# Edge set-up in parts between the pairs, more comparisons on the scalar engine, diagonals ahead: a graph layer and expert kernel

## The reference

```python
# x: 3125 x 256, src, dst: 50000 edges sorted by dst, edge_weight: 50000
def _gcn_conv(h, row, col, ew, dis, W, b):
    xw = h @ W
    norm = dis[row] * ew * dis[col]
    msg = norm[:, None] * xw[row]
    agg = jax.ops.segment_sum(msg, col, num_segments=N)
    return agg + (dis * dis)[:, None] * xw + b

x = x + gnn(layernorm(x))          # two layers: conv, layernorm, relu, residual
x = x + moe(layernorm(x))          # 16 experts, the best 2 of each row, then layernorm
```

## Time and profile before

| | us |
|---|---|
| median of 3 runs | 1250.4 (1247.85 to 1251.97) |
| profiled execution | 1253.59 |
| its span, first to last instruction | 1251.9 |
| PE busy | 1102.1 (88%) |
| DVE busy | 720.1 (58%) |
| ACT busy | 341.6 (27%) |
| POOL busy | 608.7 (49%) |

### The profile page before, as it was taken

The page is one execution under the profiler, slowest core; times in us unless marked ns, Lnnn a source line. Parts: engine busy times, 40 slices in busy tenths (PEclk is TensorE's granted clock), DMA queues, the critical chain, the costliest instruction groups (busy, mean ns, idle before and its releaser), DMA issues. The chain is left out here.

```text
span 1251.9 us, 19252 instructions
## 1 busy us (share of the span) xinstructions
PE 1102.1 (88%) x6433; PEld 952.7 (76%) x6436; DVE 720.1 (58%) x1970; ACT 341.6 (27%) x794; POOL 608.7 (49%) x625
## 2 busy tenths in 40 slices
PE   1675789799999999997799999999994599999967
PEld 1453568588888888886588888888883599999954
DVE  8978668903444444342427777777777355454536
ACT  1538332401111121111101111111211133343337
POOL 3777777777777777770001111111112355555525
PEclk9999978799999999998899999999996799999988
DMA  7999700033433433213045544535447422222236
GB/s 282 335 392 389 309 2 1 8 106 106 157 107 117 147 107 111 101 54 105 0 176 178 202 155 150 202 126 193 146 146 247 145 73 73 69 73 73 72 106 234
DMA packets 76335, 180.75 MB, mean 144 GB/s; under 512 B 28930, under 2 KB 58252, under 8 KB 66508
## 3 DMA queue, kind: packets, MB, share of 16 engines
q1 hardware_dynamic: 44984, 151.67, 33.6%
q0 software_dynamic: 19776, 15.76, 4.6%
q10 hardware_dynamic: 11476, 12.07, 3.0%
HBM read 122.12 MB, written 57.33 MB: 143 GB/s over the span
## 5 line engine op out<-in xcount | busy, mean ns | idle before, releaser
L458 POOL DMA_INDIRECT weights_by_cell<-w_cell,cell x391 | 413.0, 1056 | 140.5 <-issue 136.1
L1148 PE MATMUL ps<-x_rows,w 128*128 128x256 f32 x1300 | 296.4, 383 | 7.4 <-DMA w<-weights_by_cell 7.1
L1148 PE MATMUL ps<-w 128*128 128x256 f32 x1300 | 301.1, 385 | 1.1 <-ACT w L850 1.1
L1148 PEld LDWEIGHTS ps<-x_rows,w 128*128 128x128 f32 x1300 | 248.0, 192 | 41.2 <-DMA w<-weights_by_cell 7.9
L1148 PEld LDWEIGHTS ps<-w 128*128 128x128 f32 x1300 | 243.4, 192 | 32.7 <-ACT w L850 2.6
L508 POOL DMA_INDIRECT token_and_home_of_slot<-pair,slot_id x50 | 49.6, 992 | 346.7 <-DVE slot_id L779 339.1
L606 DVE TENSOR_TENSOR layer<-ps,w 128x1024 bf16<-128x1024 f32 x87 | 105.0, 1216 | 26.2 <-PE ps L987 26.1
L1466 DVE TENSOR_SCALAR hidt<-ps,b1t 128x128 f32<-128x128 f32 x232 | 65.3, 344 | 90.6 <-PE ps L1322 90.6
L1334 PE MATMUL ps<-w,hidt 128*128 (+1 forms) x464 | 109.8, 380 | 0.0
L1322 PEld LDWEIGHTS ps<-xt,w1s 128*128 128x128 f32 x880 | 106.9, 192 | 2.8
L1322 PE MATMUL ps<-xt,w1s 128*128 128x128 f32 x880 | 107.1, 275 | 0.0
(11 more groups left out here) (237 smaller groups left out, 1371.3 us busy)
## 6 DMA issues: line engine op xcount, KB each, us to landing
w<-weights_by_cell SPq DMA_DIRECT2D x49, 1600.0 KB, 6.9
weights_by_cell<-w SPq DMA_DIRECT2D x26, 1600.0 KB, 8.4
w<-in_L_ffn_w_dram SPq DMA_DIRECT2D x32, 512.0 KB, 8.8
weights_by_cell<-w_cell,cell POOLq DMA_INDIRECT x391
w<-in_x_dram ACTq DMA_DIRECT2D x1, 3072.0 KB
hot<-in_x_dram ACTq DMA_DIRECT2D x24, 128.0 KB, 2.1
normalised_rows<-hot ACTq DMA_DIRECT2D x24, 128.0 KB, 4.7
out_dram<-w SPq DMA_DIRECT2D x24, 128.0 KB
```

The costliest lines, as they stand in the source:

```text
L458: pool.indirect_dma_start(adj[:, :], bass.IndirectOffsetOnAxis(ap=cell[0:m, c:c + 1].bitcast(U32), axis=0), w_cell[0:m, n, half * CH + j:h ...
L1148: mm = pe.matmul(bank(k % 2, 0, D), ring[:, place_of(k), s * P:(s + 1) * P], tab[q][:, s, :], start=(s == 0), stop=(s == NT - 1))
```

## The change

- The set-up before pair 0 is for group 0 alone, after small loads of its own; the other three groups are made in 25 steps each (`part`), two steps a pair from pairs 4, 17 and 30 on. The limits are made after pair 1, and GpSimd waits for `part_ready` of the group that it scatters.
- ScalarE compares 23 pairs: 20, 24 to 44 in steps of four, and 50, 53 to 95 in steps of three (L61's rule gave 11). It has a bank of its own (2) and a fourth buffer; VectorE has two banks and three buffers. TensorE makes the key rows for ScalarE's next pair right after its present one.
- The turns and products start at s=100 (84 before), the scaling by dis at s=177, spread over the rest; the normalisation is at s=46 to 94, every fourth s.
- SP waits on the scatters' semaphores (`seconds`), not on GpSimd's count `placed`. The blank is half as long and read twice. Loads and GpSimd's first instructions are reordered.
- `combine` has twelve diagonals ahead, four in their own memory and eight in the experts' weight buffer; the gates are made in expert block 6, and in `combine` ScalarE makes halves of diagonals at 7/6 a tile.

```diff
-KBANKS = 3
+KBANKS, ACT_BANK = 2, 2
...
-ACT_FIRST, ACT_LAST, ACT_STEP = 20, 64, 4
+P_MEAN, P_PASSED, P_SHIFT, P_DEG = 14, 14, 22, HOT_LAST + 4
+T_APPLY, APPLY_STEP, T_TAB, TAB_STEP, T_DEG = 46, 4, 100, 3, 2 * P_DEG
+T_SCALE = max(2 * P_DEG + 6, T_TAB + TAB_STEP * NT + 2)
+P_GUARD = T_APPLY // 2 + 2
+
+ACT_PAIRS = tuple(range(20, 48, 4)) + tuple(range(50, PAIRED - 1, 3))
+DVE_PAIRS = tuple(p for p in range(PAIRED) if p not in ACT_PAIRS)
+SIDE, PART_OPS, PART_SPAN = 6, 24, 13
+SECONDS = 16 * (CH * ((CHUNKS + 1) // 2) - 1)


 def by_act(p):
-    return ACT_FIRST <= p < ACT_LAST and (p - ACT_FIRST) % ACT_STEP == 0
-
-
-def act_pairs(p):
-    return sum(by_act(k) for k in range(p))
+    return p in ACT_PAIRS
+
+
+def part_pair(g, j):
+
+    return 4 + (g - 1) * PART_SPAN + j // 2 + (j >= SIDE)

...
-                sp.dma_start(e_int[0:SH, 0:SG - 1, :], dst[0:full * SBE].rearrange("(g s e) -> s g e", s=SH, e=SBE)).then_inc(edges_in, 16)
+                sp.dma_start(e_int[0:SH, 0, :], dst[0:SH * SBE].rearrange("(s e) -> s e", e=SBE)).then_inc(edges_first, 16)
                 for half in range(2):
-                    sp.dma_start(e_w[half * SH:(half + 1) * SH, 0:SG - 1, :],
-                                 edge_weight[0:full * SBE].rearrange("(g s h q) -> h s g q", s=SH, h=2, q=P)[half]).then_inc(weights_in, 16)
...
-                        sp.reg_load(reg, chunks_of[0:1, t:t + 1])
-                        sp.wait_ge(placed, sp.snap(reg, min_val=1, max_val=CHUNKS + 1))
+                        for j in range(2):
+                            sp.reg_load(regs[j], second_need[0:1, j, t:t + 1])
+                        for j in range(2):
+                            sp.wait_ge(seconds[j], sp.snap(regs[j], min_val=16 * CH, max_val=SECONDS))
+                            sp.sem_inc(cells_blank, 1)
...
+                        pool.wait_ge(part_ready, (n * CH + CH - 1) // SH + 1)
                         pool.wait_ge(w_ready, n + 1)
...
-                        pool.sem_inc(placed, 1)
-                n = CHUNKS - 1
-                pool.wait_ge(seconds[n % 2], 16 * (CH * (n // 2 + 1) - 1))
-                pool.sem_inc(placed, 1)
+                pool.wait_ge(seconds[0], SECONDS)
+                pool.wait_ge(seconds[1], 16 * CH * (CHUNKS // 2))
...
-                dve.wait_ge(ends_ready, 1)
-                dve.tensor_scalar(key_part[:, :, :], e_f, MID, None, ALU.subtract).then_inc(keys_ready, 1)
-                ew = e_w.rearrange("p g q -> p (g q)")
-                dve.wait_ge(weights_in, 16 * 5)
-                link(dve.tensor_scalar(bad_e, ew, 0.0, 0.0, ALU.mult, ALU.not_equal))
-                link(dve.copy_predicated(ew, bad_e, zeros[:, :]))
-                link(dve.scalar_tensor_tensor(ew, ew, -1.0, ew, ALU.mult, ALU.max))
-                dve.tensor_scalar(ew, ew, 1e-6, None, ALU.max).then_inc(weights_ready, 1)
+                def part(g, j):
+
+                    at = (3 if g == 0 else 7) * BANK
+                    ends_ps = ps[:, at:at + 2 * P].rearrange("p (h t s) -> p h t s", h=2, t=2)
+                    dst_ps, src_ps = ends_ps[:, :, 0, :], ends_ps[:, :, 1, :]
...
+                    elif j == 17:
+                        link(dve.tensor_copy(w_parts[:, 0, cols], w_ps))
+                    elif j == 18:
+                        link(dve.tensor_tensor(rest, w_ps, w_parts[:, 0, cols], ALU.subtract))
+                    elif j == 19:
+                        link(dve.tensor_copy(w_parts[:, 1, cols], rest))
+                    elif j == 20:
+                        dve.tensor_tensor(w_parts[:, 2, cols], rest, w_parts[:, 1, cols], ALU.subtract).then_inc(cols_ready, 1)
...
-                    dve.wait_ge(keyrow_ps, p + 1)
-                    if p >= MRING:
-                        dve.wait_ge(wsum_ps, 2 * (p - MRING) + 2)
+                    d = DVE_PAIRS.index(p)
+                    dve.wait_ge(keyrow_ps, d + 1)
+                    if d >= MRING:
+                        dve.wait_ge(wsum_ps, 2 * DVE_PAIRS[d - MRING] + 2)
...
+                    for g in range(1, SG):
+                        for j in range(PART_OPS + 1):
+                            if part_pair(g, j) == p:
+                                part(g, j)
...
                 pair(1)
-                link(dve.tensor_copy(work_i[:, :], dst_c))
-                link(dve.tensor_scalar(work_i[:, :], work_i[:, :], 7, None, ALU.logical_shift_right))
-                link(dve.tensor_copy(dst_hi, work_i[:, :]))
+                limits()
                 weigh(0)
-                link(dve.scalar_tensor_tensor(dst_lo, dst_hi, -float(P), dst_c, ALU.mult, ALU.add))
+                limits_back()
+                for j in range(21, PART_OPS + 1):
+                    part(0, j)
...
                 def act_compare(p):
-                    act.wait_ge(keyrow_ps, p + 1)
-                    if act_pairs(p):
-                        act.wait_ge(same_by_act, act_pairs(p))
+                    a = ACT_PAIRS.index(p)
+                    act.wait_ge(part_ready, 2 * p // SH + 1)
+                    act.wait_ge(keyrow_act, a + 1)
+                    if a:
+                        act.wait_ge(same_by_act, a)
                     for k in range(2):
                         for half in range(2):
...
-                    act.activation(same[:, p % MRING, :, :, :].rearrange("p s h q -> p (s h q)"),
+                            act.activation(key_gap[:, k, half, :], bank(ACT_BANK, k * SBE, (k + 1) * SBE), ACT.Abs,
+                                           bias=key[:, c:c + 1], scale=-1.0).then_inc(apart, 1)
+                    act.wait_ge(apart, 4 * (a + 1))
+                    if a:
+                        act.wait_ge(wsum_ps, 2 * ACT_PAIRS[a - 1] + 2)
+                    act.activation(same[:, MRING, :, :, :].rearrange("p s h q -> p (s h q)"),
                                    key_gap.rearrange("p s h q -> p (s h q)"), ACT.Relu, bias=ones_f[:, 0:1], scale=-1.0).then_inc(same_by_act, 1)
...
                         if t > 0:
                             take_product(t - 1)
...
+                    if s >= T_SCALE:
+                        if s == T_SCALE:
+                            act.wait_ge(dis_ready, 1)
+                            act.wait_ge(prod_read, NT)
+                        for t in range((s - T_SCALE) * NT // (SBS - T_SCALE), (s + 1 - T_SCALE) * NT // (SBS - T_SCALE)):
                             act.activation(tab[0][:, t, :], tab[0][:, t, :], ACT.Copy, scale=dis[:, t:t + 1]).then_inc(tab_ready[0], 1)

...
+                def next_key_rows(p):
+
+                    wait_same(p)
+                    if by_act(p):
+                        a = ACT_PAIRS.index(p) + 1
+                        if a < len(ACT_PAIRS):
+                            key_rows(ACT_PAIRS[a], ACT_BANK, keyrow_act)
+                    else:
+                        d = DVE_PAIRS.index(p) + KBANKS
+                        if d < len(DVE_PAIRS):
+                            key_rows(DVE_PAIRS[d], d % KBANKS, keyrow_ps)
+                    if p == ACT_PAIRS[0] - 4:
+                        key_rows(ACT_PAIRS[0], ACT_BANK, keyrow_act)
...
+                    p = s // 2
+                    slot = MRING if by_act(p) else DVE_PAIRS.index(p) % MRING
...
+                    if s % 2 == 0:
+                        next_key_rows(s // 2)
                     weigh(s)
+                    if s == CH - 1:
+                        limits()
...
                     with act.If(more(act, "act")):
                         for b in range(usual + 2, BLOCKS):
                             next_block(b)
+                        act.wait_ge(h_ps, BLOCKS)
+                        act.wait_ge(w1_ready, BLOCKS - FIXED)
                     act.wait_ge(gate_set, 1)
                     for t in range(DIAGS):
+                        if t == OWN_DIAGS:
+                            act.wait_ge(h_ps, usual + 1)
+                            act.wait_ge(w1_ready, usual + 2 - FIXED)
                         for k in range(2):
-                            ins = act.activation(diag[:, t, k, :], ident[:, :], ACT.Copy, scale=top_w[:, k, t:t + 1])
+                            ins = act.activation(diag(t, k), ident[:, :], ACT.Copy, scale=top_w[:, k, t:t + 1])
...
                         add_out(b, b % 2)
+                        if b == RARE:
+                            dve.wait_ge(exp_ready, 1)
+                            link(dve.tensor_scalar(top_w[:, 0, :], eg[:, :], 1.0, None, ALU.add))
+                            link(dve.reciprocal(top_w[:, 0, :], top_w[:, 0, :]))
+                            dve.tensor_tensor(top_w[:, 1, :], top_w[:, 0, :], eg[:, :], ALU.mult).then_inc(gate_set, 1)
...
+    def halves_by(t):
+
+        return min(t * 7 // 6, 2 * (NT - DIAGS))

...
+                for j in range(halves_by(t), halves_by(t + 1)):
+                    d, k = DIAGS + j // 2, j % 2
+                    act.wait_ge(y_ps, d - DIAGS + 1)
```

(34 more changed lines are left out.)

290 lines of the change are left out of this document (157 added, 133 removed).

## The result

The changed kernel takes **1260.4 us** (median of four runs, 1257.4 to 1262.2); the kernel before, measured beside it, 1250.5. The ratio is 1.008, with a 95% interval of 1.006 to 1.010: slower, by 8 to 12.5 us. The forecast was 1253, with a range of 1237 to 1262, so the time lies in the range, but of the cases it is that of the slower one, C. The profiled execution is the shortest of the four: 1257.4 us for a span of 1255.8, with a mean granted clock of 0.94; the other three have 0.90 to 0.91.

The account below looks back on a forecast made before the run. Bounds: VectorE, then TensorE's handshake with ScalarE in the edge stage; GpSimd's scatters at tile 24; ScalarE in the tail. Profiled 1253.6, +6.8 at tile 25, -3.8 tail, gives 1256.6, less 3.2: 1253 us; range 1237 to 1262.

Parts of the forecast that it names:

- C: Edge stage: idle gaps keep TensorE at 1.2 GHz, end 272 to 276, total 1257 to 1261 us; chance 0.33.
- Prologue: Start: setting up one column group first brings first comparison to 15.6, pair 2 to 23.4, 8.7 us earlier.
- Parts between the pairs: Edge stage: the other three groups' 75 VectorE instructions between pairs cost 20.8 us, bounds 16 and 24.
- Pairs 2 to 49: Edge stage: VectorE's work and waits, 128.9 us, put pair 49 at 152.3; TensorE reaches pair 50 at 155.1.
- Pairs 50 to 79: Edge stage: TensorE idles behind ScalarE's comparisons; three pairs take 7.48 us warm, 9.8 cold; a quarter cold adds 5.5.
- B: Edge stage: ScalarE's comparisons hidden, end by 250, GpSimd becomes the bound at tile 24, total 1236 us; chance 0.17.
- D: Edge stage: parts at 16 us and no hold-up, end 254, total 1239 to 1246 us; chance 0.15.
- Pairs 80 to 97: Edge stage's end: after product 24, ScalarE alone sets 5.95 us for three pairs; end 262.5 with a warm clock.
- Border 2: Tile 24 of layer 1: GpSimd ends 8.1 us earlier, no wait, tile 25 starts 6.8 us later.
- Tail: Last stage: fewer half diagonals make a tile 0.93 us instead of 1.17; sum -3.8 us, bounds -4.5 and -2.
- The shift of -3.2: Whole kernel: the sum, made against the profiled 1253.6 us, is shifted by -3.2 at the end for the median.
- A: Edge stage: balance, the forecast itself; end 262 to 269, total 1247 to 1254 us; chance 0.35.

Follow-up runs that it names:

- e1: The changed kernel, but ScalarE compares only the seven pairs 20 to 44 and VectorE all from 50 on: 1242.9 us.
- e10: e1 with a wait added: for pairs 50 to 79 VectorE starts a comparison only when TensorE has weighed the pair before: 1248.1 us.
- e4: The changed kernel with the diagonals as before, four in advance and two halves a tile in the last stage: 1259.3 us.
- e2: The changed kernel with ScalarE's comparisons from pair 53 on four sub-blocks earlier in its order, ahead of the product: 1230.9 us.
- e7: e2, but SP waits for GpSimd's report of a chunk as before, not the scatters' own semaphores: 1229.5 us.
- e6: e2 with every second pair from 20 to 48 compared on ScalarE, 15 in place of 7: 1227.8 us.
- e5: e2 with the diagonals as before, four in advance and two halves a tile in the last stage: 1231.6 us.
- e8: The kernel before, with ScalarE comparing up to pair 48 only, no longer 52, 56 and 60: 1255.7 us.

## Why the prediction was right, and where it was not

*Prologue.* The mechanism was right, the times too late by 2 us: the first comparison came at 13.7 for 15.6, pair 2 at 21.4 for 23.4. The price of the hold-up (3 us) was about right: L579 took 2.85 and the next such instruction 0.23, so 2.6.

*Parts between the pairs.* Counted at 20.8 us; their 75 instructions took 0.22 to 0.32 each, and 19.3 from each start to the next. Their other side was missed: GpSimd has more scatters done there. From 30 to 60 before and after:

```profile
30.00:60.00 30.00, 21.94 (x15) 1.00 0.87 318
```

```profile
30.00:60.00 30.00, 23.61 (x20) 1.00 0.92 293
```

A scatter took 1.46 us there and now 1.18. That it is the short waits between the parts' chained instructions that let GpSimd through fits e1 and e10, but no run tries it in this stretch, where the blanking was changed as well.

*Pairs 2 to 49.* Here the count failed most. VectorE starts pair 49 at

```profile
139.18 1.22 DVE L655 TENSOR_TENSOR layer<-ps,w 128x1024 bf16<-128x1024 f32 x1
```

and not at 152.3: 117.7 us behind pair 2, not 128.9. Of the 11.2 us too many, the largest step is "add the 7.4 in which it waits for the prefix products": the products were ready, with 0.2 us of idle time, in the grouped rows of VectorE from 21.4 to 139.2.

```profile
L731 DVE TENSOR_TENSOR w<-w,ps 128x512 f32<-128x512 f32 (+1 forms) x7 | 4.4, 628 | 0.2
```

With the 1 us taken for key rows the waits were counted at 8.4, and the rows with an idle time show 0.6. The parts took 19.3 in place of 20.8, and the other work 97.9 in place of 99.7. So TensorE reached pair 50 at 142.2, not 155.1, 12.9 us sooner than counted:

```profile
142.23 0.60 PE L1044 MATMUL ps<-key_part,pick 128*128 128x256 f16 x2
```

*Pairs 50 to 79.* The mechanism and both periods were right (7.48; 9.8 counted, 10.06 measured). Mis-sized was the share of them at the lower clock: "a quarter in the new periods adds 5.5" was carried over from before (and a quarter of ten periods at 2.3 each would be 5.8). The ten periods from pair 50 to pair 80, at 235.7, took 93.5 us, not 80.3. One of them is the warm 7.48, and the lower clock and its way in add 18.7 to the ten, not 5.5. The errors of 12.9 and 13.2 cancel: the start of layer 1, 268.4 for 268.0, was right by luck. In e4's trace, with the same edge stage, it is 261.5. With a warm clock it would by these numbers have been near 250 (an estimate: 268.4 less 18.7) and the kernel faster than before, as cases B and D had it. That the lower clock came with the gaps is shown by e2, which has neither, and by the thirteen traces listed under e4; how many periods fall to it is not settled by the program.

*Pairs 80 to 97.* 32.6 counted, 32.7 measured.

*Border 2.* No wait, tile 25 6.5 later (6.8 counted). But "GpSimd ends 8.1 earlier" was 19.8: the lead is 9.2 at the first scatter, 15.8 at the 31st (82 us before, 67 now), and grows again from 12.1 at the 101st, behind 178 us, to 18.3 at the 141st, where VectorE before had no gap. It cost the forecast nothing, since TensorE came later still. It did spoil rival B, priced at 1236 with tile 24 at 561.9: e2, which is B made true, has tile 24 at 550.9 and takes 1230.9. The new SP waits have no visible part in that (e7). "Nothing, but up to 7 if the stage were 15 us quicker" for the table behind the blanking became 7.85 in e6.

*Tail.* -3.8 counted. From before to after the traces have -2.0: +0.1 ahead of the last block (0.5 counted), and -2.1 behind it (4.3 counted). A tile in the middle takes 0.88 us, for 0.93 forecast, but ScalarE waits longer for VectorE's statistics at the first and last tiles, as the prediction feared: 8.3 us in all where it was 6.2, of that 0.98 at the last root. The twelve diagonals alone are worth 1.35 in the traces and nothing that the times could tell (e4, e5).

*The shift of -3.2.* It took the profiled execution for as long above the median as before. This one lies 3.0 below. Without that term the forecast is 1256.6, and the profiled execution took 1257.4. The clock differs from run to run (0.90 to 0.94), and probably with it the number of long periods; only one of the four has a trace.

So the case whose mechanism and time came true is C: ScalarE's comparisons behind the product, with TensorE at 1.2 GHz for most of the stretch. Its own mark, an end past 269, was not reached in the trace, because pair 50 came 12.9 us sooner than counted; that the forecast of A, 1253, is only 7 us off is in part owed to this. The rule for the whole kernel is in the table: tile 24 begins 4.0 to 4.8 us behind the last scatter, or, where layer 1 begins later than some 239 (550.2, which is the last scatter's 545.9 and 4.3, less the 311.6 that the tiles take), without a wait. The later of the two sets the time: from there to the end of the span all thirteen traces of the table take 675 to 682 us.

## What to carry to other kernels

When work goes to another in-order engine, look at what stands in front of it in that engine's own order: the same comparisons cost 29 us more behind the product than ahead of it. When two chains meet late (here TensorE's tiles and GpSimd's scatters), price a change on both, for the one that it speeds up may slow the other. An idle gap of 1.5 us in 7.5 costs more than itself when TensorE's clock falls with it: here some 14 us of gaps came with 19 of clock.

## What was unexpected in the hardware

- GpSimd's indirect DMA takes 0.97 us, but 1.4 to 1.9 where VectorE goes from one instruction to the next without a gap: one per comparison. In e8 this outweighed a faster edge stage. That it is the one-hots with two SBUF inputs, and not the comparisons, which hold it up is read from the timeline and was not tried by itself.
- TensorE stayed at 1.2 GHz for 61 us while busy for 87% of them, its idle times 1.33 to 1.35 us; in e2, without these, it had 2.4 GHz throughout the same pairs. With the same gaps e4 had 0.72 on the mean.
- The key rows at 142.23 took 0.60 us, as at the lower clock (0.39 at 158.06), where the column of the granted clock reads 1.00. From 80 to 140 they take 0.59 to 0.63 in all of five traces looked at, and the column reads 1.00 in three (after, e2, e10) and 0.50 in two (e1, e6). So ahead of pair 50 the column doesn't tell how fast TensorE is, and by its durations it is slow there in all of them; from 160 on column and durations agree.
- On one chip the kernel before took 1597.5 us in place of 1250.
